# Token rows kept as two fp16 halves, and turned by transposing DMA instead of TensorE

## The reference, cut to what matters

```python
x1 = x + attention(layernorm(x)) @ W_out + b_out
z  = layernorm(x1)
xn = layernorm(z) * gamma + beta
w, idx = top_k(softmax(xn @ gate_w), 2)            # 8 experts, 2 for a token
h = gelu(xn @ w1[e] + b1[e]);  y_e = h @ w2[e] + b2[e]   # hidden width 1024
out = x1 + z + sum over the chosen e of w_e * y_e
```

## Time and profile before

| | |
|---|---|
| median of three runs | 970.12 us |
| profiled execution | 971.45 us, span 969.7 us, mean granted clock 0.927 |
| PE busy | 852.3 us, 88% |
| DVE busy | 719.4 us, 74% |
| ACT busy | 586.3 us, 60% |
| POOL busy | 480.5 us, 50% |

### The profile page before, as it was taken

How to read it: one execution, slowest core, us unless ns; L and a number is a source line. 1 busy time by engine, 2 the same in 40 slices (tenths; PEclk the granted TensorE clock), 3 DMA queues, 4 the chain that set the end, 5 groups by cost and what they waited for, 6 DMA issues and landing times.

```text
span 969.7 us, 21171 instructions
## 1 busy us (share of the span) xinstructions
PE 852.3 (88%) x6870; PEld 573.6 (59%) x6870; DVE 719.4 (74%) x1594; ACT 586.3 (60%) x1079; POOL 480.5 (50%) x574
## 2 busy tenths in 40 slices
PE   4899977868788879688887899989999999999996
PEld 3555522323353425243333688879888999989875
DVE  6677888867649697988975679875776776666664
ACT  1767466645758687877867474555544554455453
POOL 4000023333536666767586748774476554454441
PEclk9899988777979889988897999989999999999999
DMA  9788657745757768467725652342323332323231
GB/s 202 240 288 272 224 168 221 213 108 160 196 145 215 195 174 236 136 186 190 220 80 158 216 130 40 57 94 40 53 39 59 51 57 45 52 47 49 40 52 18
DMA packets 146326, 130.09 MB, mean 134 GB/s; under 512 B 59344, under 2 KB 128848, under 8 KB 146096
## 3 DMA queue, kind: packets, MB, share of 16 engines
q1 hardware_dynamic: 115648, 87.51, 32.1%
q0 software_dynamic: 15680, 18.95, 12.1%
q10 hardware_dynamic: 14896, 22.28, 7.2%
HBM read 83.63 MB, written 44.80 MB: 132 GB/s over the span
## 4 chain that ended last, share of the span: by engine, by line
PE 42%; DVE 16%; POOL 12%; DMA 11%; issue 10%; SPq 6%; ACT 2%; POOLq 1%; ACTq 0%; DVEq 0%
PE banks L774 13%; PE banks L792 12%; PE banks L587 5%; POOL slot_tokens L1659 4%; POOL out L1712 3%; PE banks L702 3%; DMA weighed_values<-arena 3%; DVE arena L1235 3%; PE banks L690 2%; POOL arena L1688 2%; PE banks L577 2%; DVE weights L1392 2%; DVE arena L1077 2%; DMA inverse_sums<-arena 2%; PE banks L646 2%
## 5 line engine op out<-in xcount | busy, mean ns | idle before, releaser
L996 ACT ACTIVATE arena<-banks,arena 128x256 f32<-128x256 f32 (+1 forms) x312 | 152.5, 541 | 171.3 <-issue 124.3
L774 PE MATMUL banks<-arena,weights 128*128 128x256 f16 (+1 forms) x1872 | 204.2, 265 | 2.5 <-DVE arena L1494 1.9
L792 PE MATMUL banks<-weights,arena 128*128 x1704 | 196.2, 275 | 0.5 <-DVE arena L1522 0.5
L1712 POOL DMA_INDIRECT out<-arena x71 | 116.3, 1638 | 152.1 <-DVE arena L1533 114.2
L774 PEld LDWEIGHTS banks<-arena,weights 128*128 x1872 | 173.9, 98 | 27.9 <-issue 4.3
L792 PEld LDWEIGHTS banks<-weights,arena 128*128 128x128 f16 x1704 | 167.1, 99 | 21.6 <-issue 1.1
L646 PE MATMUL banks<-arena 64*128 64x128 f16 (+3 forms) x512 | 118.5, 329 | 32.5 <-DMA arena<-arena 12.2
L618 PE MATMUL banks<-arena 62*128 62x384 f16 (+3 forms) x512 | 95.0, 327 | 38.2 <-DVE arena L1232 12.3
L1520 DVE TENSOR_SCALAR arena<-arena 128x512 f16<-128x512 f32 (+1 forms) x156 | 75.7, 485 | 59.0 <-ACT arena L996 57.2
L1522 DVE SCALAR_TENSOR_TENSOR arena<-arena 128x512 f16<-128x512 f32 (+1 forms) x156 | 110.0, 705 | 5.6
L646 PEld LDWEIGHTS banks<-arena 64*128 64x128 f16 x512 | 38.3, 99 | 115.2 <-issue 37.1
(11 more groups left out here) (191 smaller groups left out, 1374.1 us busy)
## 6 DMA issues: line engine op xcount, KB each, us to landing
weights<-in_L_ffn_w ACTq DMA_DIRECT2D x16, 1024.0 KB, 7.8
arena<-in_L_ffn_w SPq DMA_DIRECT2D x32, 512.0 KB
qk_parts<-weights SPq DMA_DIRECT2D x64, 128.0 KB
arena<-qk_parts SPq DMA_DIRECT2D x128, 64.0 KB, 3.5
weighed_values<-arena SPq DMA_DIRECT2D x32, 256.0 KB
token_rows<-arena SPq DMA_DIRECT2D x12, 512.0 KB, 5.1
arena<-qk_parts SPq DMA_DIRECT2D x128, 32.0 KB, 3.6
arena<-weighed_values SPq DMA_DIRECT2D x32, 128.0 KB
```

The costliest lines, as they stand in the source:

```text
L774: m = pe.matmul(bank[:, c * TILE:c * TILE + WIDTH[j]], w1[:, k, wp, f:f + P], xp[:, k, 0:WIDTH[j]], start=(i == 0), stop=(i == len(terms) ...
L792: m = pe.matmul(bank[:, c * D:(c + 1) * D], hp[:, f, c * P:(c + 1) * P], w2[:, f // (FC // 2), wp, f % (FC // 2), :], start=(f == 0 and i ...
L996: m = act.activation(h_32[r % 2][:, c, 0:WIDTH[j]], banks[:, 1 + c2, c * TILE:c * TILE + WIDTH[j]], ACT.Gelu, bias=b1_now[j % 2][:, 2 * c2 ...
L1712: g.indirect_dma_start(acc_dram[:, :], bass.IndirectOffsetOnAxis(slot_of(j, c), 0), y[j % 2][:, c, :], None, compute_op=ALU.add).then_inc( ...
```

## The change

Token rows are now multiplied by the fp16 scale `SCALE_X` before they are stored (`gamma` and `beta` are scaled once, `gate_w` is divided by it once). A stage `row_high` on ACT rounds the rows of a batch to fp16, `row_low` makes the remainder (on POOL for batches 0 to 5, on DVE for 6 and 7), both in the tile `x2`, and `rows_out` stores `x2`: for each token 256 high and 256 low fp16 values, the same bytes as before. Since `x2` is then in use until it is stored, `load_again` and `with_bias` work in `rows`, and `add_out` writes `x2`. In the expert stage SP turns a gathered chunk, 128 tokens x 512 fp16 values, with one transposing DMA into `xt`, high and low halves together; PE's `turn`, ACT's `turn_high` and DVE's `turn_low` are gone, and DVE keeps only the weights (`share`).

```diff
+        row_high, row_low = (x2[:, :, i * D // 2:(i + 1) * D // 2].bitcast(F16) for i in range(2))
...
-            at(base + 142, "load_again", b)
+            at(base + 166, "load_again", b)
...
-            at(base + 326, "rows_out", b)
+            at(base + 336, "row_high", b)
+            at(base + 344, "row_low", b)
+            at(base + 348, "rows_out", b)
...
-                at(base, "turn", j + 1)
+                at(base - 8, "turn", j + 1)
...
-                at(base + 3, "turn_high", j + 1)
-                at(base + 5, "turn_low", j + 1)
+                at(base + 5, "share", j + 1)
...
# PE
-            def turn_tokens(j): ... pe.transpose(...)
-                w.wait_ge(sem("xt_low"), j + 1)        # in hidden
+                w.wait_ge(*xt_in(j))
...
# ACT
-                if b > 0:                               # in scale_rows
-                    w.wait_ge(sem("rows_out"), 16 * b)
-                    w.wait_ge(sem("side_made"), side_made("turn_x", (b - 1, 1)))
+            def split_rows(b):
+                w.wait_ge(sem("beta_added"), b + 1)
+                w.wait_ge(sem("acc_out"), 16 * (b + 1))
+                act.copy(row_high, rows).then_inc(sem("row_high"), 1)
-            def turn_high(j): ...
...
# DVE
+                v.tensor_scalar(gamma, gamma, SCALE_X, None, ALU.mult)
+                v.tensor_scalar(beta, beta, SCALE_X, None, ALU.mult)
+                v.tensor_scalar(gate_w, gate_w, S_UNDO[:, 2:3], None, ALU.mult).then_inc(sem("x_scaled"), 1)
+                if b > 0:                               # in add_out
+                    w.wait_ge(sem("rows_out"), 16 * b)
+            def split_rows(b):                          # batches 6 and 7
+                w.wait_ge(sem("row_high"), b + 1)
+                both(row_low, rows, row_high, ALU.subtract).then_inc(sem("row_low"), 1)
...
# POOL
+                elif stage == "row_low" and n < B - 2:
+                    w.wait_ge(sem("row_high"), n + 1)
+                    g.tensor_tensor(row_low, rows, row_high, ALU.subtract).then_inc(sem("row_low"), 1)
-                    w.wait_ge(sem("x_turned_2"), j - 2) # in gather
+                    w.wait_ge(*xt_in(j - 3))
...
# SP
             def load_again(b):
                 if b > 0:
-                    w.wait_ge(sem("acc_out"), 16 * b)
+                    w.wait_ge(sem("side_made"), side_made("turn_x", (b - 1, 1)))
+                    w.wait_ge(sem("row_low"), b)
+            def turn_tokens(j):
+                w.wait_ge(*gathered_in(j))
+                if j >= 2:
+                    w.wait_ge(sem("hidden"), FC // 2 * (j - 1))
+                else:
+                    w.wait_ge(sem("scored_T"), BANKS_A_UNIT * UNITS)
+                for c in range(CHUNKS[j]):
+                    sp.dma_start(xt[j % 2][:, :, c * P:(c + 1) * P], gathered[j % 3][:, c, 0:D].bitcast(F16),
+                                 transpose=True).then_inc(sem(f"xt_in{j % 2}"), 16)
-                    w.wait_ge(sem("beta_added"), n + 1) # in rows_out
+                    w.wait_ge(sem("row_low"), n + 1)
```

More of the change, by code:

```diff
@@ L261, in build @@
         a4 = Area(arena, HEAD, STACKS_END)
+        a4.at = -(-HEAD // 8) * 8
         gathered = [a4.take(TC * ROW, c=TC, d=ROW) for _ in range(3)]
         assert a4.at <= HEAD + 2 * 2 * (HQ * T // 2)
-        xt_high = [a4.take(KC * TILE // 2, F16, k=KC, s=TILE) for _ in range(2)]
-        xt_low = [a4.take(KC * TILE // 2, F16, k=KC, s=TILE) for _ in range(2)]
+        xt = [a4.take(2 * KC * TILE // 2, F16, k=2 * KC, s=TILE) for _ in range(2)]
         h_32 = [a4.take(2 * TILE, c=2, s=TILE) for _ in range(2)]
@@ L522, in gathered_in, with xt_in @@
             return sem(f"gathered{j % 3}"), 16 * sum(CHUNKS[j % 3:j + 1:3])
+        def xt_in(j):
+            return sem(f"xt_in{j % 2}"), 16 * sum(CHUNKS[j % 2:j + 1:2])
         def x_rows(b):
@@ L730, in count @@
                 m.then_inc(sem("side_made"), 1)
[L732 to L742, removed]
             expert_of = {}
@@ L821, in tensor @@
                     count(n)
-                elif stage == "turn":
-                    turn_tokens(n)
                 elif stage == "hidden":
@@ L977, in load_late @@
                 act.dma_start(w_16[:, e_, m_, k_, :, :], late_dram[i]).then_inc(sem(f"late_in{m_}"), 16)
-            def turn_high(j):
-                w.wait_ge(sem("x_turned_2"), j + 1)
-                if j >= 2:
-                    w.wait_ge(sem("hidden"), FC // 2 * (j - 1))
-                else:
-                    w.wait_ge(sem("scored_T"), BANKS_A_UNIT * UNITS)
-                act.activation(xt_high[j % 2][:, :, 0:WIDTH[j]],
-                               banks[:, 0, :].rearrange("p (k s) -> p k s", k=KC)[:, :, 0:WIDTH[j]], ACT.Copy,
-                               scale=SCALE_X).then_inc(sem("xt_high"), 1)
             def gelu(j, c2):
@@ L1062, in scalar @@
                     act.activation(Q_TMP[:, 0:1], Q_TMP[:, 0:1], ACT.Gelu)
-                elif stage == "turn_high":
-                    turn_high(n)
+                elif stage == "row_high":
+                    split_rows(n)
                 elif stage == "gelu":
@@ L1249, in add_out @@
                 w.wait_ge(*side_out("out_proj", (b, half)))
-                own_x = x2[:, 2 * half:2 * half + 2, :]
-                v.tensor_tensor(own_x, turned[:, half, :].rearrange("p (s d) -> p s d", s=2), own_x,
+                if b > 0:
+                    w.wait_ge(sem("rows_out"), 16 * b)
+                else:
+                    w.wait_ge(sem("v_store1"), 16 * (B // 2))
+                own_x = slice(2 * half, 2 * half + 2)
+                v.tensor_tensor(x2[:, own_x, :], turned[:, half, :].rearrange("p (s d) -> p s d", s=2), rows[:, own_x, :],
                                 ALU.add).then_inc(sem("out_added"), 1)
@@ L1592, in vector @@
                     stage_bias(n)
-                elif stage == "turn_low":
-                    turn_low(n)
+                elif stage == "row_low" and n >= B - 2:
+                    split_rows(n)
+                elif stage == "share":
+                    shares_of(n)
                 elif stage == "split_hidden":
@@ L1728, in gpsimd @@
                     w.wait_ge(sem("vectors_in"), 96)
-                    g.tensor_tensor(x2, x2, over_tiles(b_out), ALU.add).then_inc(sem("with_bias"), 1)
+                    g.tensor_tensor(rows, rows, over_tiles(b_out), ALU.add).then_inc(sem("with_bias"), 1)
                 elif stage == "gamma" and n < B - 2:
                     w.wait_ge(sem("rows_scaled"), n + 1)
+                    w.wait_ge(sem("x_scaled"), 1)
                     m = own.mark(g.tensor_tensor(rows, rows, over_tiles(gamma), ALU.mult))
@@ L1932, in sync @@
                     load_late(n, *splits[n])
+                elif stage == "turn":
+                    turn_tokens(n)
                 elif stage == "table":
@@ L1947, in sync @@
                 elif stage == "rows_out":
-                    w.wait_ge(sem("beta_added"), n + 1)
+                    w.wait_ge(sem("row_low"), n + 1)
                     sp.dma_start(rows_dram[n * T:(n + 1) * T, 0:D].rearrange("(t p) d -> p t d", p=P),
-                                 rows).then_inc(sem("rows_out"), 16)
+                                 x2).then_inc(sem("rows_out"), 16)
                 elif stage == "shares_out":
```

17 lines of the change are left out of this document (7 added, 10 removed).

## The result

The changed kernel took 977.18 us in the median of five runs, the kernel before 970.12 us beside it: ratio 1.009, 95% interval 1.0056 to 1.0124 (the two medians alone are 1.007 apart). Forecast was 964 us. It is slower, and the sign was wrong. One of the five runs took 1314.47 us and is left out of the ratio. The profiled execution took 976.19 us (span 974.4), 4.7 us more than the profiled one of before, and that difference is what is taken apart here.

What follows compares the result with a forecast made beforehand. PE was taken to bound the expert stage, with no engine full in attention. Terms -15.2 - 2 + 6.5 + 5 = -5.7 us on the profiled 971.45 gave 965.7, as a median 964; own range 957 to 971.

Steps and rivals of the forecast that it cites:

- X: Expert stage: time from a gather's landing to its transposed tile being ready, put at 4 to 5 us and hidden.
- the budget: Expert stage: a wide tile's transposes have 9.0 us from landing to landing before PE waits; gain gone at 10.3.
- the prediction's own sign: Expert stage: a transpose's issue-to-landing time of about 3 us would be right, 5 or more wrong.
- The turns, -15.2: Expert stage: PE's turns disappear, 32 wide tiles at 0.43 us and 7 narrow at 0.23, saving 15.2 us.
- The late gather, -2: Expert stage: of one 3.51 us wait for late rows, 2 us come back, between 0 and 6.
- Attention, +6.5: Attention stage: added ACT work, POOL work and late x together cost 6.5 us, between 0 and 17.
- ACT's 4 us: Attention: row_high and a store wait add 10 us of ACT, of which 4 us were let through.
- the late x: Attention: x arrives up to 2.8 us late, holding up POOL and DVE; 5.7 us for four later batches.
- the 2.5: Attention: the part of DVE's 5.7 us delay from x arriving late that gets through, 2.5 us.
- Handover, +5: Attention to experts: hidden(0) waits for a transpose on SP's crowded queue, costing 5 us, between 1 and 10.
- Attention and handover pay in full: Rival: ACT's 10 us, DVE's 5.7 and 9 at the handover, 24.7 instead of 11.5, giving 977; chance 0.20.

Runs made afterwards that it cites:

- tiny low part: Changed kernel with row_low's subtraction on 8 elements a partition, transposes reading fp16 weights: ratio 1.0017 to the kernel before, last scores at 532.9 us.
- Low part first: Changed kernel with row_low moved in the order from tick 344 to 339 for batches 0 to 5, ahead of the divide: ratio 1.0017 to the kernel before.
- high part tiny: Changed kernel with ScalarE's row_high cast on 8 elements a partition, transposes reading fp16 weights: ratio 1.0119 to the kernel before, 978.65 us.
- x loaded once: Changed kernel with x loaded again for batch 0 only, later batches adding the bias to what is in rows: ratio 0.9996 to the kernel before.
- both parts tiny: Changed kernel with row_high and row_low on 8 elements a partition, waits and transfers kept, transposes reading fp16 weights: ratio 0.9982 to the kernel before.
- own buffer: Changed kernel with x loaded early into x2, row_high in separate space, row_low in place over rows, two stores: ratio 0.9969 to the kernel before.
- own buffer with late weights on ScalarE: Changed kernel with x, high and low parts in separate buffers, and SyncE's half of the last weight loads issued by ScalarE: ratio 0.9960 to the kernel before.
- expert part alone: Changed kernel with attention as before the change, transposing transfers reading fp16 weights instead of gathered rows: ratio 0.9895 to the kernel before.
- changed kernel of set 2: The changed kernel run again, unaltered, beside the kernel before in another set of runs: ratio 1.0000, last scores at 542.6 us.

## Why the prediction was wrong

The sum was -15.2 - 2 + 6.5 + 5. Measured in the profiled pair: -10.9 (both expert terms) + 10.3 + 5.3 = +4.7. Two small slips are in the sum itself: without the first wide turn, 15.4 is 15.0 and not 15.2, and 5.1 + 2.5 us against 5.2 makes x 2.4 us late and not 2.8.

**X and the transposes: hidden, as forecast, with X too small.** X was put at 4 to 5 us and is 5.4 to 6.3, still under the 9.0 of the budget; the wide tile takes 10.48 us as forecast. By the prediction's own sign, 5 us or more from issue to landing would be wrong, and with SyncE's issuing it is 5.2 and 6.2. The Trainium skill's block price (VectorE: DVE Perf Modes, section The three transpose paths), an estimate of 10.5 us for a wide tile if its eight blocks run one behind the other, doesn't hold here. A tile's two transfers had landed 5.4 to 6.3 us after the gather, issue included, and apart from the late gather the stage paid only with them run twice. What no term had was SyncE's 1.2 us to issue one, about a fifth of X.

**The turns, -15.2: right for the wide tiles, 3 us too large in all.** By the starts of the hidden groups, the last 18 wide tiles took 196.8 us before and 188.6 after, the 0.43 us each and a little more. The first 14, beside `place`, took 173.1 and 170.0: 3.1 saved of 6.0, and 1.5 of the difference is the late gather below. The seven narrow tiles with the end took 57.5 and 58.0, so their 1.6 us were not saved. The prediction had seen that only 0.06 us were left behind a narrow turn, had named up to 7 x 0.23 us to give back, and counted nothing for it. That the split is what filled the place isn't shown: the one named wait there is 0.72 us for a transposed chunk, and the rest is spread over the hidden groups.

**The late gather, -2: failed.** Two us were to come back; the wait grew from 3.51 to 5.02 us instead. POOL's queue of `place` decides when that gather is issued, and behind it now stand X = 5.4 us. The term had the wrong sign, and its bounds of 0 to 6 didn't allow for that.

**Attention, +6.5: the step that failed, with 10.3.** In five profiles of the new attention part against three of the old it is nearer 15 (542.1 and 527.1 in the mean), inside the bounds of 0 to 17. What failed in it is above all one sentence: "It stands just before `divide`, for whose input POOL idled six times, 25.4 us in all; that idle covers it: nothing". row_low was read one place too early. It stands at tick 352 (base 8 + 344), the divide at 348, so the idle time lies ahead of the divide and the work behind it, ahead of a mask that PE needs. The tiny low part put this at 7 to 10 us, and the one moved line gives 7.2 us of the total back. ACT's 4 us, on the other hand, show nowhere: the high part tiny gained nothing (its wait for the store, 3.8 us in three, stays in that run). Of the late x, VectorE's waits were larger than forecast (11.0 us in five, against 5.7), and what reached the last scores, 2 to 5 us with x loaded once, holds the 2.5. The same 8 ticks were missed there too: load_again stands at 350 in rows_out's count, 2 ticks behind it and not 10. Some 6 us of attention remain with both parts tiny. The late x is still in that run, and own buffer, which takes it out and keeps the arithmetic, ended its last scores 7.4 us before the changed kernel of its set; the two together would account for the whole, but no run has both.

**Handover, +5: right in size (5.3), not in its parts.** It was argued from a crowd on SyncE's queue that holds the transposes back. They were issued as soon as the gather had landed, and two runs that took SyncE's loads away from ahead of them gained about 1 us at most. The crowd shows in how long the two transfers took, 7.51 and 7.71 us. That the size came out is partly luck.

**The chances.** The time of 977 is that of the rival "Attention and handover pay in full", but not by its sum: the handover cost the forecast's 5 us and not 9, ScalarE's 10 us weren't paid, and instead the expert stage gave 6.3 us less than counted. That its number fits is chance.

No version that computes the whole is faster than the kernel before by the 0.5% that can be told. Low part first is level with it (1.0017, 0.9991 to 1.0044) and faster than the changed kernel; own buffer with late weights on ScalarE had 0.9960 (0.9935 to 0.9985) in a set where the changed kernel had 1.0000. The expert part alone has shown 0.9895. To get there, the low part would have to stand ahead of the divide and x come early at once, which none of these kernels has: it needs one more buffer of 256 KB than was found, and is untried.

## What to carry to other kernels

Idle time of an in-order engine covers only work that stands ahead of the instruction that waits. Before you write "nothing" beside an added instruction, write out its two neighbours in the order and see on which side the wait lies; that is a subtraction of two ticks. A saving on the bounding engine holds only in the tiles where nothing else is due: check the margin of each shape and count the ones with none as zero. And where every stage stands at a base plus a tick, add the base before you compare: 8 ticks left out put the low part on the wrong side of the divide.

## What the runs showed of the hardware

A transposing transfer of 128 rows of 512 fp16 values (128 KB) from SBUF to SBUF kept SyncE for 1.25 us at the median (1189 to 3224 ns in 71 of them) where a plain store of rows took 0.37. With 71 of them the packets of the whole run went from 146326 to 184950. PE kept its 10.48 us a tile beside them, at a DMA share of 0.53.

Two transfers that took 4.05 and 4.04 us in the expert stage, a gather of rows and a transposing transfer of them, took 7.51 and 7.71 us at the handover, where six loads of 512 KB were under way beside them.

The granted clock of the attention window fell from 0.85 to 0.83 while PE's busy time there stayed (321.76 and 320.90 us, 61 matmuls fewer inside the window). The change isn't shown as its cause: the window has 0.85 in the changed kernel of set 2 and 0.83 with the expert part only, behind the old attention part.

The kernel before ran at 967 to 970 us in three sets and at 987 to 989 in two, with PE pauses called "issue", 11 to 15 us of the 20, as the visible difference. The changed kernel's ratio was 1.000 in one of the latter and 1.008 and 1.009 in the former. What causes the pauses was not tried.
